# Tree weights fetched one tree further ahead, one row or column fewer for the inner nodes, and the first add of X one scan step sooner

## The reference

```python
# layer 0
xn = layernorm(x); s = attention(xn)                # 16 heads, 4 groups
g = silu(mixture_of_experts(xn))                    # 64 experts, top 8
x = x + s * g
# layer 1
xn = layernorm(x)
s = mamba(xn)                                       # selective scan: 512 channels x 16 states
g = silu(tree_ffn(xn))                              # below
x = x + s * g

def tree_ffn(x):                                    # 8 trees of depth 7, 255 nodes each
    logits = x @ W_in.T + b_in
    # each tree: start at the root, go right where the logit is > 0; keep silu(logits) of the 8
    # nodes on the path and nothing of the others (masked)
    return masked.reshape(B, 8 * 255) @ W_out.T

def selective_scan(...):                            # for each channel and state, over time
    ht = exp(dt * A) * ht + dt * B_t * x_t
    y_t = sum over states of ht * C_t
```

## Time and profile before

| what | value |
|---|---|
| median of 3 runs | 2938.65 us (2933.99 to 2943.05) |
| the profiled execution | 2938.65 us |
| its span, first to last instruction | 2936.8 us |
| granted TensorE clock, mean | 0.924 of full speed |
| TensorE busy | 2444.6 us, 83% |
| VectorE busy | 1980.5 us, 67% |
| ScalarE busy | 1847.6 us, 63% |
| GpSimd busy | 1732.7 us, 59% |
| DMA of SP's queue (q1), share of 16 DMA engines | 16.9% |
| DMA of GpSimd's queue (q0), share of 16 DMA engines | 32.7% |

### The profile page before, as it was taken

One profiled execution on the slowest core, in us unless ns is written; L12 is line 12 of the kernel. 1 busy time (PEld: TensorE's weight loads), 2 busy tenths in 40 slices (PEclk: granted clock), 3 DMA queues, 4 the chain that ended last, 5 costly groups with the idle time before them and its releaser, 6 DMA issues.

```text
span 2936.8 us, 37630 instructions
## 1 busy us (share of the span) xinstructions
PE 2444.6 (83%) x12740; PEld 1379.8 (47%) x12744; DVE 1980.5 (67%) x2957; ACT 1847.6 (63%) x3346; POOL 1732.7 (59%) x1416
## 2 busy tenths in 40 slices
PE   5777779998789989898989898988898889877772
PEld 3444457764434454445444454445444544453331
DVE  4778845543356767676767666766776677669897
ACT  3456724446476775777667766775677567756762
POOL 1000064407757786877687658766886597636565
PEclk9888889999899999998999898999999999998896
DMA  4000178854555565654664455436543654357776
GB/s 146 22 19 5 30 205 238 248 168 67 96 118 104 106 141 129 122 100 104 145 118 100 94 143 113 84 78 160 112 96 76 155 116 88 81 120 170 168 167 145
DMA packets 282177, 344.96 MB, mean 117 GB/s; under 512 B 66177, under 2 KB 211535, under 8 KB 281985
## 3 DMA queue, kind: packets, MB, share of 16 engines
q0 software_dynamic: 84224, 176.19, 32.7%
q1 hardware_dynamic: 175248, 144.80, 16.9%
q10 hardware_dynamic: 22512, 21.57, 2.2%
HBM read 198.23 MB, written 26.80 MB: 77 GB/s over the span
## 4 chain that ended last, share of the span: by engine, by line
PE 40%; ACT 15%; DVE 14%; issue 14%; POOL 13%; DMA 2%; SPq 1%; POOLq 0%; ACTq 0%; DVEq 0%; another core or an unknown queue 0%
PE bank L1764 6%; PE bank L1753 6%; POOL arena L1644 5%; PE bank L1715 4%; PE bank L1900 4%; POOL acc_sb L1622 4%; PE bank L1929 4%; PE bank L1874 4%; DVE bank L1533 4%; PE bank L1822 3%; ACT PT L1019 2%; PE bank L1776 2%; ACT Pr L999 2%; POOL arena L1660 2%; POOL arena L1650 2%
## 5 line engine op out<-in xcount | busy, mean ns | idle before, releaser
L1644 POOL TENSOR_TENSOR arena<-arena 128x512 f32<-128x512 f32 x512 | 856.4, 1742 | 16.1 <-DVE arena L1524 16.1
L1650 POOL TENSOR_TENSOR arena<-arena 128x512 f32<-128x512 f32 x192 | 275.1, 1433 | 396.0 <-DVE arena L1533 395.7
L1622 POOL DMA_INDIRECT acc_sb<-ybuf,slot_idx x256 | 422.1, 1649 | 145.4 <-DMA ybuf<-arena 63.7
L1228 DVE TENSOR_REDUCE negmax<-bank 128x1 f32<-128x512 f32 x512 | 340.5, 679 | 246.8 <-PE bank L1753 245.9
L1136 ACT ACTIVATE bank<-arena,A_sb 128x512 f32<-128x512 f32 x512 | 355.2, 697 | 207.4 <-DVE arena L1538 168.9
L1764 PE MATMUL bank<-ident,Pr 128*128 128x128 f32 x2048 | 349.2, 296 | 128.3 <-ACT PT L1019 64.6
L1753 PE MATMUL bank<-Kp,Qp 64*128 64x512 f32 x1024 | 403.3, 678 | 63.1 <-ACT Pr L999 58.4
L999 ACT ACTIVATE Pr<-bank,negmax 128x512 f32<-128x512 f32 x512 | 353.1, 690 | 150.7 <-DVE negmax L1228 149.0
L1533 DVE TENSOR_TENSOR_SCAN bank<-bank,arena 128x512 f32<-128x512 f32 x320 | 390.6, 1221 | 68.4 <-ACT bank L1136 55.8
L1019 ACT COPY PT<-bank 128x512 f32<-128x512 f32 x512 | 300.3, 587 | 186.9 <-PE bank L1764 181.5
L1764 PEld LDWEIGHTS bank<-ident,Pr 128*128 128x128 f32 x2048 | 226.0, 146 | 305.3 <-issue 101.5
(11 more groups left out here) (212 smaller groups left out, 3874.6 us busy)
## 6 DMA issues: line engine op xcount, KB each, us to landing
arena<-arena POOLq DMA_DIRECT2D x256, 512.0 KB, 5.1
arena<-bc_dram SPq DMA_DIRECT2D x256, 256.0 KB, 3.8
ybuf<-arena ACTq DMA_DIRECT2D x64, 256.0 KB, 4.8
arena<-in_w_gate SPq DMA_DIRECT2D x64, 128.0 KB, 3.1
arena<-in_w_up SPq DMA_DIRECT2D x64, 128.0 KB, 3.9
arena<-in_w_down SPq DMA_DIRECT2D x64, 128.0 KB, 4.7
arena<-in_X SPq DMA_DIRECT2D x8, 512.0 KB, 7.3
s_sb<-in_X SPq DMA_DIRECT2D x8, 512.0 KB, 7.1
```

The lines of the kernel that those rows point to most:

```text
L1228: dve.tensor_reduce(negmax[:, m % RING_STAT:m % RING_STAT + 1], bank[m % RING_S_ATT][:, :], AX.X, ALU.max, negate=True).then_inc(att_max, 1)
L1622: pool.indirect_dma_start(acc_sb[:, i, :], None, ybuf, bass.IndirectOffsetOnAxis(ap=slot_idx[:, b * TILES + i, k:k + 1], axis=0), bounds_c ...
L1644: pool.tensor_tensor(st_sb[:, g % RING_S, :], u_sb[:, size_slot(b, cb), :], B_sb[:, load % RING_BC, :], ALU.mult).then_inc(ssm_input, 1)
L1650: pool.tensor_tensor(v, v, C_sb[:, load % RING_BC, :], ALU.mult).then_inc(ssm_c_pool, 1)
```

## The change

Three edits. In `inputs`, the first half's `cmb_add` moves ahead of the yield after the second gate, one scan step sooner. In `tree_w`, the half of the inner nodes loads 127 columns of ffn_WinT (or 127 rows of ffn_WoutT) instead of 128. In `tree_a` and `tree_b`, SP is told to load the weights of tree r+4 (in) and r+2 (out) where it was r+3 and r+1; the semaphore values that the loads wait for are the same functions of the tree.

```diff
@@ inputs
         for half in range(2):
             E.cmb_gate(b, half)
+            if half:
+                E.cmb_add(b, 0)
             yield 0
         done["gated"] = b + 1
-        for half in range(2):
-            E.cmb_add(b, half)
+        E.cmb_add(b, 1)
@@ tree_w
-                for half in range(2):
+                for half, m in enumerate((INNER, P)):
                     lo = r * NODES + half * INNER
                     if kind == "in":
-                        sp.dma_start(tree_in[place][half], ffn_WinT[:, lo:lo + P].rearrange("(c p) n -> p c n", p=P)).then_inc(tree_in_w[place], 16)
+                        sp.dma_start(tree_in[place][half][:, :, 0:m], ffn_WinT[:, lo:lo + m].rearrange("(c p) n -> p c n", p=P)).then_inc(tree_in_w[place], 16)
                     else:
-                        sp.dma_start(tree_out[place][half], ffn_WoutT[lo:lo + P, :]).then_inc(tree_out_w[place], 16)
+                        sp.dma_start(tree_out[place][half][0:m, :], ffn_WoutT[lo:lo + m, :]).then_inc(tree_out_w[place], 16)
@@ tree_a, tree_b
-                if r >= 1 and r + RING_W - 1 < TREES:
-                    self.tree_w(b, "in", r + RING_W - 1)
+                if r + RING_W < TREES:
+                    self.tree_w(b, "in", r + RING_W)
-                if 2 <= r + 1 < TREES:
-                    self.tree_w(b, "out", r + 1)
+                if 2 <= r + 2 < TREES:
+                    self.tree_w(b, "out", r + 2)
```

## The result

The changed kernel takes 2992.58 us (median, 2991.06 to 2997.2) against 2939.63 us for the kernel before: ratio 1.0181, 95% interval 1.0162 to 1.0201. It is 53 us slower. The direction was forecast and the range held it, but the forecast of 168 us was three times the size.

What follows compares the result with a forecast made beforehand. No engine fills the kernel: a chain between engines waiting for each other's small pieces bounds it. 8 batches x 21 = 168 us, order's 10 us falling on rows already late, add 0: 2938.65 + 168 = 3107 us; range 2965 to 3280.

Steps and rivals of the forecast that it cites:

- The queue's order: SP's weight loads moved one tree ahead: no gain, B rows held behind them, 10 us for the order alone.
- 127 rows through one engine: Inner half of each out load: 127 rows pass one DMA engine, as the path load did; 9.3 us per half.
- The price of a kilobyte: Time of 1 KB on one DMA engine in the tree stages: 73 ns, with GpSimd's queue holding a third.
- the prediction's low bound: 1 KB on one DMA engine alone takes 49 ns; batch 0's product needing B row 2 is then 4.7 us late.
- the central 16: Batch 0's trees: at 73 ns a kilobyte, the product needing B row 2 would be 16 us late.
- Batch 0, step by step: Chain of loads on one engine from out 2's half to B row 2, ending at 850.4 against 834.3: 16 us late.
- the sum for a batch is 21 us: Each batch's tree stage: 16 us late at B row 2 plus 5 us from out 5, 6 and 7; 4.7 to 41.
- Rival (b): All hidden: late B rows cost only time in which GpSimd waits for the scan anyway; 2939 us, chance 0.08.
- a rival that makes the kernel faster: Part of TensorE's issue idle before line 1900 is an unnamed wait for weights; a tenth gone gives 2925 us, chance 0.04.
- The add: GpSimd's first add of X one scan step sooner: gain at most 3.3 us, cost up to 8, taken as 0.
- The signs named beforehand: Out halves and B, C rows landing in 8 us or more, GpSimd waiting for B, long SP issues, other stretches unchanged.

Runs made afterwards that it cites:

- The delays with and without lead: Kernel before, GpSimd's product with B done four extra times at one step per batch, far ahead of the scan (ratio 1.0068) or least ahead (1.0156).

## Why the prediction was right in kind and wrong in size

**The queue's order.** Right. The order of SP's issues came out as derived, and the order alone cost 3 us, not 10. B row 115, read off as 5.6 us late, was 6.1 us late with the order alone, but VectorE did not wait longer for it, for the reason below. That one ring's descriptors are taken in order the Trainium skill (DMA: Bandwidth & Descriptors) says in "Queues, rings and completion order", not in the section that the prediction names. This trace agrees: after tree 2's 127 rows, from 841.7 us on, the one engine moves 8 packets of 1 KB, 32 of half a KB, 8 of 2 KB and then 1 KB again, the order of issue.

**127 rows through one engine.** Right, and the single largest part: 39 of the 53 us go when it is taken out, and splitting the load takes the cost away with no byte less. The rows of the path load were the trace's whole evidence, and it was enough.

**The price of a kilobyte.** Wrong, and made up for by a second error. 73 ns was taken, with a third added for GpSimd's queue. The rows above give 42 ns for a packet of 1 KB, with that queue silent or at 75.5%. In batch 0, the chain of 3 x 127 + 88 = 469 KB begins at 832.9 (816 and the 17 us) and the product that waits for its end starts at 862.5, 29.6 us later. Of these, 3.4 pass before the first of the 127 rows moves and some 3.2 in the two stretches of 4 packets; the other 23.0 are 49 ns a KB, the prediction's low bound. At 49 ns it had 4.7 us of lateness; with the 6.6 us of pauses, which it did not have, that is the 11 us measured. That the central 16 came near was luck.

**The step that failed** is the one from a late B row to time: "Batch 0, step by step", where lateness was measured against the start of the product that needs the row, and "the sum for a batch is 21 us", where that lateness was taken as time lost. Batch 0 lost nothing and no batch lost 21 us; all eight lost 47 to 49 in the two profiles, not 168. GpSimd makes its products a median of 8.7 us ahead of the scan in batch 0, 12.8 at the product in question (it ends at 835.9, its scan starts at 848.7). The need is the scan's, so the row had some 22 us to spare and not 9.7. Rival (b) said this and was given 0.08; its evidence stood in the earlier trace rows, a GpSimd that waits 4.29 us for the scan just before the product "in need". In the whole run GpSimd waits 186 us for rows and 156 us less for VectorE. The delays with and without lead show the same by a cause put in by hand: 20 against 45 us. Where the lead is short, the prediction's step holds; it was wrong to take it for every row.

**What was left out.** The weights that land late cost about 20 us of the 127 rows' 33 in the old order. The prediction named weights only as a rival that makes the kernel faster. It put four trees, 29 us, between their landing and their use. In the changed kernel TensorE waits 3.1 us for them, since out r+2 is issued a tree sooner. So the order helps where the prediction saw no gain, and the price is paid in C and B rows instead (VectorE's 54 us).

**The add.** Put at 0 between -3.3 and +8; alone it costs 11 us. The bound took the wait at the gate, and not that GpSimd's products are pushed beside a gate that they slow. Some 20 us of these waits and 9 us of slower gates stand beside the 11; which of them it is, no run parts.

**The signs named beforehand.** GpSimd waits for B rows: seen. Long issues after an out load: seen. Landing of the 127-row halves: the profile gives none for them. B and C rows at over 8 us: only the longest (11.6; the median is 4.2), since the hold is at issue, before the landing is counted. Stretches outside the trees as long as before: the experts' stage was not, by the chip and not by the change.

## What to carry to other kernels

Look at the row count of each DMA: one of 127 rows held the queue that issues it for up to 11.6 us, and everything behind it, while 128 rows, or 120 and 7, cost nothing; here to load one row that nobody reads is the simplest way. Measure the slack of a load not against the instruction that reads it but against the first engine behind it that has nothing else to do: an engine that runs ahead absorbs much of a lateness until its lead is used up. And look on both sides of a moved instruction for what it pushes together on two engines.

## What the runs showed of the hardware that was not expected

A queue is held at issue around a load of 127 rows: 8.08 us for a pair of loads on SP, 9.75 us for one on ScalarE, 6.56 us at the program's start. It is held even where the one engine has nothing to do (834.1 to 836.2 us). A VectorE product of two SBUF operands took 3.57 us instead of 0.66 while GpSimd ran two products of the same kind. The experts' stage, bound by its loads and TensorE, takes 233 or 247 us with the same instructions, the clock granted at 0.95 or 0.92.
